# A macaron block of two feed-forward layers and a scan: the opening in another order

## The reference

```python
def ffn(x):                                   # weights w1, w2, h1, h2, w3 hold -1, 0 and 1
    h = silu(tlin(x, w1, s1)) * tlin(x, w2, s2)          # 128 -> 512
    h = gelu(tlin(h, h1, sh1), approximate=False)        # 512 -> 512
    h = gelu(tlin(h, h2, sh2), approximate=False)        # 512 -> 512
    return tlin(h, w3, s3)                               # 512 -> 128
x = x + 0.5 * ffn(layernorm(x))
x = x + attn(layernorm(x))                    # h_t = tanh(B x_t + A h_(t-1)), then C and W_out
x = x + 0.5 * ffn(layernorm(x))
```

## Time and profile before

| | |
|---|---|
| median of 3 runs | 384.37 us (384.05 to 384.40) |
| the profiled execution | 384.28 us, its span 382.4 us |
| granted clock of TensorE | 0.999 over the span |
| PE busy | 375.9 us, 98% of the span |
| DVE, ACT, POOL busy | 279.6, 267.7, 163.7 us |
| moved by DMA | 14.02 MB over the span |

### The profile page before, as it was taken

One profiled execution on the slowest core, in us unless ns is written; L12 is line 12 of the kernel. 1 busy time (PEld: TensorE's weight loads), 2 busy tenths in 40 slices (PEclk: granted clock), 3 DMA queues, 4 the chain that ended last, 5 costly groups with the idle time before them and its releaser, 6 DMA issues.

```text
span 382.4 us, 6587 instructions
## 1 busy us (share of the span) xinstructions
PE 375.9 (98%) x1793; PEld 299.9 (78%) x1793; DVE 279.6 (73%) x724; ACT 267.7 (70%) x625; POOL 163.7 (43%) x156
## 2 busy tenths in 40 slices
PE   7999999999999999999999999999999999999995
PEld 6877777778788787878778788888888788887774
DVE  5978989797777777576868866777767677686713
ACT  3899495768758688576685767858576775757654
POOL 3645362645526355242551633535334352533421
PEclk9999999999999999999999999999999999999999
DMA  7920000000000000000001001010100101000001
GB/s 228 433 112 1 27 2 27 2 2 28 2 28 0 2 27 0 28 2 28 27 2 56 2 18 39 0 55 2 46 9 0 55 0 55 0 29 27 2 28 33
DMA packets 6366, 14.02 MB, mean 37 GB/s; under 512 B 1088, under 2 KB 2112, under 8 KB 6080
## 3 DMA queue, kind: packets, MB, share of 16 engines
q1 hardware_dynamic: 5328, 13.37, 9.2%
q10 hardware_dynamic: 1008, 0.29, 0.3%
HBM read 7.37 MB, written 2.10 MB: 25 GB/s over the span
## 4 chain that ended last, share of the span: by engine, by line
PE 85%; issue 7%; POOL 3%; ACT 3%; DVE 2%; POOLq 0%; DVEq 0%
PE F L274 66%; PE FR L274 7%; PE FR L302 2%; PE SC L491 2%; POOL y_lo L1489 1%; PE SC L422 1%; POOL y_lo L1495 1%; PE F L519 1%; PE FR L292 1%; ACT y_hi L1216 1%; PE SC L274 1%; ACT y L1213 1%; PE MI L302 1%; PE F L521 1%; PE MI L282 1%
## 5 line engine op out<-in xcount | busy, mean ns | idle before, releaser
L274 PE MATMUL F<-y_hi,w_hi 128*128 128x512 f32 (+1 forms) x484 | 196.7, 407 | 0.3 <-DVE y_lo L1045 0.2
L274 PE MATMUL F<-y_lo,w_hi 128*128 128x512 f32 (+1 forms) x484 | 188.5, 390 | 0.0
L274 PEld LDWEIGHTS F<-y_hi,w_hi 128*128 128x128 f32 x484 | 91.0, 188 | 20.6 <-issue 2.2
L1213 ACT ACTIVATE y<-F,sc 128x512 f32<-128x512 f32 x111 | 76.1, 685 | 41.4 <-PE F L274 40.3
L274 PEld LDWEIGHTS F<-y_lo,w_hi 128*128 128x128 f32 x484 | 91.2, 188 | 15.9
L837 DVE TENSOR_TENSOR y_lo<-y,y_hi 128x512 fp32r<-128x512 f32 x79 | 64.9, 821 | 39.1 <-ACT y_hi L1216 39.1
L1489 POOL TENSOR_TENSOR y_lo<-y,y_hi 128x512 fp32r<-128x512 f32 x48 | 66.7, 1396 | 59.3 <-DVE y_hi L824 48.6
L1495 POOL TENSOR_TENSOR y_lo<-y,y_hi 128x512 fp32r<-128x512 f32 x48 | 62.5, 1308 | 34.8 <-ACT y_hi L1216 34.5
L1216 ACT ACTIVATE y_hi<-F,sc 128x512 fp32r<-128x512 f32 x111 | 76.0, 684 | 0.0
L1232 ACT ACTIVATE h<-SC 128x32 fp32r<-128x32 f32 x96 | 18.7, 195 | 47.9 <-PE SC L437 46.9
L274 PE MATMUL F<-xn_hi,w_hi 128*128 128x512 f32 x118 | 49.5, 420 | 0.1
(11 more groups left out here) (170 smaller groups left out, 438.4 us busy)
## 6 DMA issues: line engine op xcount, KB each, us to landing
x_all<-in_xT SPq DMA_DIRECT2D x1, 2048.0 KB, 15.6
x_all<-x1c SPq DMA_DIRECT2D x8, 256.0 KB, 2.3
x_all<-lnin SPq DMA_DIRECT2D x8, 256.0 KB, 2.2
out<-outb SPq DMA_DIRECT2D x7, 256.0 KB, 2.0
x_all<-in_xtok SPq DMA_DIRECT2D x1, 1536.0 KB, 11.4
w_raw<-in_h1T SPq DMA_DIRECT2D x2, 512.0 KB, 6.9
w_raw<-in_h2T SPq DMA_DIRECT2D x2, 512.0 KB, 8.2
x_all<-in_xtok SPq DMA_DIRECT2D x2, 128.0 KB, 2.6
```

The costliest lines, as they stand in the source:

```text
L274: mm = nc.tensor.matmul(out, wtile(w, layer, k, m), y, start=first and i == 0, stop=last and i == len(pairs) - 1)
L1213: nc.scalar.activation(y23[:, m, :], bankt[:, :], ACT.Gelu, scale=s)
```

## The change

Six things change, all of them in the opening.

- The number of zero matmuls, WARM, goes from 19 to 15.
- w1 and w2 are laid out by output tile, tile m of w1 beside tile m of w2, in one array w12T. Its first piece is now 256 columns (m = 0), its second the other 768. `wtile` finds the tiles there.
- The second half of chunk 0 is loaded by ACT's queue, ahead of ACT's small loads. Three small loads that the scan needs (`a_raw`, `b_rep`, `mask`) go from ACT's queue to the end of SP's.
- On DVE, `count(0)` goes from ahead of chunk 0's normalisation to behind it, and `count(1)` from ahead of `xn_lo` to behind chunk 1's statistics.
- On ACT, only piece 0 is cast ahead of `xn_hi`; piece 1 is cast behind it in two parts; the cast of h1's first half goes behind the first tanh, that of h1's second half behind chunk 1's normalisation.
- On POOL, `w_lo` of layer 1 is made in three parts (256, 256 and 512 columns) as the casts arrive, where it was two parts of 512.

```diff
-WARM = 19
+WARM = 15
...
-        PIECES = [(0, HID), (HID, HID)] + [(WOFF[2] + i * HALF, HALF) for i in range(4)] + [(WOFF[4], KT * P)]
+        PIECES = [(0, 2 * P), (2 * P, 2 * HID - 2 * P)] + [(WOFF[2] + i * HALF, HALF) for i in range(4)] + [(WOFF[4], KT * P)]
...
         def wtile(w, layer, k, m):
 
+            if layer < 2:
+                off = (2 * m + layer) * P
+                return w[:, off:off + P]
...
-                pe.wait_ge(w_hi_ready, 2)
+                pe.wait_ge(w_hi_ready, 1)
                 pe.wait_ge(xn_hi_r, 1)
...
             first_layer1()
+            pe.wait_ge(w_lo1_ready, 2)
             layer1(0, 1, True)
-            pe.wait_ge(w_lo1_ready, 2)
+            pe.wait_ge(w_lo1_ready, 3)
             layer1(0, 2, True)
...
             first_layer2(1)
+            pe.wait_ge(w_hi_ready, 5)
             first_layer2(2, range(KT - 1))
...
-            count(0)
             dve.wait_ge(rstd["f"], 1)
...
-            count(1)
+            count(0)
             dve.wait_ge(xn_hi_r, 1)
...
             first_stats(1)
             mean_negated(1)
+            count(1)
             count(2)
...
+            act.dma_start(xt_all[:, N // 2:N], xtok[:, N // 2:N]).then_inc(ld_x0[1], 16)
             act.dma_start(ident[:, :], ident_d).then_inc(ld_id, 16)
...
-            act.dma_start(a_raw[:, :], Ablk).then_inc(ld_scan, 16)
-            act.dma_start(b_rep[:, :], Brep).then_inc(ld_scan, 16)
-            act.dma_start(mask[:, :], mask_d).then_inc(ld_scan, 16)
...
             hi_part(0)
-            hi_part(1)
             act.wait_ge(feat_first, 1)
...
-            hi_part(2)
+            hi_part(1, slice(0, 2 * P))
+            hi_part(1, slice(2 * P, None))
...
             layer1(0, 0)
-            hi_part(3)
+            hi_part(2)
             layer1(0, 1)
...
             normalise(1, beside_normalisation)
+            hi_part(3)
             layer1(0, 3)
...
-            for half in range(2):
...
-                pool.tensor_tensor(part[0], part[1], part[2].bitcast(F32), ALU.subtract).then_inc(w_lo1_ready, 1)
+            for i, (lo, hi) in enumerate(((0, 2 * P), (2 * P, 4 * P), (4 * P, 2 * HID))):
+                pool.wait_ge(w_hi_ready, i + 1)
+                pool.tensor_tensor(w_lo[:, lo:hi], w_raw[:, lo:hi], w_hi[:, lo:hi].bitcast(F32),
+                                   ALU.subtract).then_inc(w_lo1_ready, 1)
...
-            for i in range(2):
-                sp.dma_start(xt_all[:, i * N // 2:(i + 1) * N // 2], xtok[:, i * N // 2:(i + 1) * N // 2]).then_inc(ld_x0[i], 16)
-            for i, (w, lo, hi) in enumerate(((w1T, 0, HID), (w2T, 0, HID), (h1T, 0, HALF), (h1T, HALF, 2 * HALF),
-                                             (h2T, 0, HALF), (h2T, HALF, 2 * HALF), (w3T, 0, KT * P))):
+            sp.dma_start(xt_all[:, 0:N // 2], xtok[:, 0:N // 2]).then_inc(ld_x0[0], 16)
+            for i, (w, lo) in enumerate(((w12T, 0), (w12T, 2 * P), (h1T, 0), (h1T, HALF), (h2T, 0), (h2T, HALF), (w3T, 0))):
...
             sp.dma_start(x_all[:, :], xT).then_inc(ld_xall, 16)
+            sp.dma_start(a_raw[:, :], Ablk).then_inc(ld_scan, 16)
+            sp.dma_start(b_rep[:, :], Brep).then_inc(ld_scan, 16)
+            sp.dma_start(mask[:, :], mask_d).then_inc(ld_scan, 16)
```

More of the change, by code:

```diff
@@ L56, in wait, with build @@
     engine.wait_ge(sem, value)
-def build(nc, xT, xtok, w1T, w2T, h1T, h2T, w3T, scales, Ablk, Brep, CTrep, WoutT, ident_d, mask_d, outT):
+def build(nc, xT, xtok, w12T, h1T, h2T, w3T, scales, Ablk, Brep, CTrep, WoutT, ident_d, mask_d, outT):
     with ExitStack() as ctx:
@@ L549, in first_turn @@
                 layer1(1, 1, gen)
-                pe.wait_ge(w_hi_ready, len(PIECES) - 1)
+                pe.wait_ge(w_hi_ready, len(PIECES))
                 pe.wait_ge(w3_hi_ready, 1)
@@ L1378, in count, with hi_part @@
                                      accum_out=ne_cnt[:, i:i + 1]).then_inc(ne_act, 1)
-            def hi_part(i):
-                off, width = PIECES[i]
+            def hi_part(i, cut=slice(None)):
                 act.wait_ge(ld_w[i], 16)
+                lo, hi, _ = cut.indices(PIECES[i][1])
+                off, width = PIECES[i][0] + lo, hi - lo
                 nc.scalar.copy(w_hi[:, off:off + width], w_raw[:, off:off + width]).then_inc(w_hi_ready, 1)
+            act.dma_start(xt_all[:, N // 2:N], xtok[:, N // 2:N]).then_inc(ld_x0[1], 16)
             act.dma_start(ident[:, :], ident_d).then_inc(ld_id, 16)
@@ L1537, in _ @@
             pool.wait_ge(normed["f"], 1)
-            pool.wait_ge(ld_w[0], 16)
-            pool.wait_ge(ld_w[1], 16)
-            pool.wait_ge(w_hi_ready, 2)
-            for half in range(2):
-                part = [w[:, 0:WOFF[2]].rearrange("p (l n) -> p l n", l=2)[:, :, half * HID // 2:(half + 1) * HID // 2]
-                        for w in (w_lo, w_raw, w_hi)]
-                pool.tensor_tensor(part[0], part[1], part[2].bitcast(F32), ALU.subtract).then_inc(w_lo1_ready, 1)
+            for i, (lo, hi) in enumerate(((0, 2 * P), (2 * P, 4 * P), (4 * P, 2 * HID))):
+                pool.wait_ge(w_hi_ready, i + 1)
+                pool.tensor_tensor(w_lo[:, lo:hi], w_raw[:, lo:hi], w_hi[:, lo:hi].bitcast(F32),
+                                   ALU.subtract).then_inc(w_lo1_ready, 1)
             inverse_std("f", 1, mv_f, ve_f, rs_f)
@@ L1550, in _ @@
             with pool.If(is_general != 0):
-                pool.wait_ge(w_hi_ready, len(PIECES) - 1)
+                pool.wait_ge(w_hi_ready, len(PIECES))
                 pool.wait_ge(w3_hi_ready, 1)
@@ L1598, in _ @@
                 off, width = PIECES[i]
-                sp.dma_start(w_raw[:, off:off + width], w[:, lo:hi]).then_inc(ld_w[i], 16)
+                sp.dma_start(w_raw[:, off:off + width], w[:, lo:lo + width]).then_inc(ld_w[i], 16)
             sp.dma_start(xt_all[:, 2 * N:], xtok[:, 2 * N:]).then_inc(ld_x, 16)
             sp.dma_start(x_all[:, :], xT).then_inc(ld_xall, 16)
+            sp.dma_start(a_raw[:, :], Ablk).then_inc(ld_scan, 16)
+            sp.dma_start(b_rep[:, :], Brep).then_inc(ld_scan, 16)
+            sp.dma_start(mask[:, :], mask_d).then_inc(ld_scan, 16)
             def save_x1(k):
@@ L1662 @@
         "xtok": np.ascontiguousarray(x.reshape(CHUNKS, QT, P, P).transpose(2, 0, 1, 3)).reshape(P, -1),
-        "w1T": tiles(v["ffn_w1_w"]), "w2T": tiles(v["ffn_w2_w"]), "h1T": tiles(v["ffn_h1_w"]),
+        "w12T": np.ascontiguousarray(np.stack([tiles(v[n]).reshape(P, KT, P) for n in ("ffn_w1_w", "ffn_w2_w")],
+                                              axis=2)).reshape(P, -1),
+        "h1T": tiles(v["ffn_h1_w"]),
         "h2T": tiles(v["ffn_h2_w"]), "w3T": tiles(v["ffn_w3_w"]),
```

## The result

The changed kernel takes 385.74 us (385.24 to 386.68, 15 runs), the kernel before 384.37 (383.46 to 385.17, 15 runs): the ratio is 1.0041, 95% interval 1.0030 to 1.0051. It is slower by 1.4 us; the forecast was 384.5 and its range ended at 385.1. The profiled execution took 385.53 us with a span of 383.2.

The account below looks back on a forecast made before the run. PE, busy 98% of the span, is gated at L742 by `ne_sum`, which DVE's and ACT's queues set. 0.07 (Step 2) + 0.14 (Step 3) = 0.2 us later, so 384.5 us forecast, range 383.9 to 385.1.

Parts of the forecast that it names:

- Step 1: Start of layer 1: earlier normalisation and fewer zeros end `xn_hi` at 8.36, 0.8 us sooner, bounds 0.4 to 0.9.
- The zeros' term: PE's opening: four fast zero matmuls fewer free PE 0.92 us sooner, at 7.17; 0.85 of it taken.
- The input's landing: Chunk 0's first half, both halves issued at once: lands 0.05 us later, bounds no change to 0.45.
- Step 2: DVE's queue up to the first gate: `count(1)` adds 0.87 us, so the gate comes at 12.45, 0.07 later.
- Step 3: ACT's queue from first `y_hi` to last count: cast adds 0.94 us, 0.80 absorbed, leaving 0.14 (0.04 to 0.24).
- Step 4: PE: waits about 0.7 us within layer 2 for the third `y`, and another 0.4 at L742 for `ne_sum`.
- The gain coming through: Rival, 5%: the 0.8 us of the earlier layer 1 start reaches the end, giving 383.5.
- The clock's rival: TensorE's pace falls at PE's wait for `xn_hi` after fewer zeros: 1.3 us later, 385.6; chance 5%.
- late input: First half lands as late as the second, 0.45 us on Step 1: 384.9 to 385.0; some 15%, within the range.

Follow-up runs that it names:

- scales_behind: The changed kernel with the three small DVE instructions on the scales put behind chunk 0's normalisation and `count(0)`, no transfer moved; 385.18 us, 1.0019 to the kernel before.
- before_scales_late: The kernel before with the load of the scales issued behind ct and wout on ACT's queue, fourth instead of second; 385.47 us, ratio 1.0040.
- one_queue: The changed kernel with the second half of chunk 0 back on SP's queue, behind the first; 384.78 us, 1.0008 to the kernel before.
- casts_back: scales_behind with the casts of h1's two halves back in their earlier places; ran once, only its trace used: ACT 8.20 us against 8.28.
- before_15_zeros: The kernel before with 15 multiplications of zeros instead of 19, nothing else; 383.89 us, ratio 0.9992.
- scales_first: The changed kernel with the load of the scales issued first on ACT's queue, ahead of chunk 0's second half; 385.69 us, 1.0033 to the kernel before.

## Why the prediction was wrong

**Step 1 failed.** The prediction had the normalisation start at 6.25 "with the count behind it", and `xn_hi` end at 8.36. It names `rs_f` and `count(0)` as what DVE waits for, and overlooks what stands between the statistics and the normalisation in the same queue: `s1h`, s3h and s12h, which wait for the scales. Before, that wait was over at 4.0 and invisible. The change moves the scales behind 128 KB on ACT's queue, and the prediction, though it followed the input's half and the three scan loads, never asked what was queued behind the half. Of the 0.92 by which the normalisation came later than forecast (7.17), `rs_f` explains 0.23 (6.44 instead of 6.21) and the wait on the scales the other 0.69. `xn_hi` ended at 9.07: 0.71 late. scales_behind and before_scales_late show the wait from both sides, and one_queue shows that the second queue makes it.

**The zeros' term was mis-sized too, hidden behind that.** Step 1 had the four zeros that go as fast ones, so that PE would be free at 7.17. In the changed kernel's trace the last of the 15 starts at about 7.23, so PE is free at about 7.46, which the late normalisation hides; in one_queue PE is free only at 7.81, and there it counts. So this term was 0.3 to 0.6 short in these two traces. That the zeros last longer in one execution than in another isn't in the prediction.

**The input's landing was mis-sized.** 0.05 was taken, with 0.45 as bound; the statistics started 0.31 later (3.70), and in the other kernels with the half first on ACT's queue from 3.87 to 3.98, against 3.15 to 3.56 in the kernels with both halves on SP's queue. The rule of the Trainium skill that was weighed there (DMA: Bandwidth & Descriptors, "Issuing engines are not separate DMA queues": transfers of several issuing engines share the 16 engines, so a second queue only saves issue time) was the better guide: the second half landed at 3.84, no sooner than before, and the first at 3.65. The same page of the Trainium skill ("Queues, rings and completion order") says that an engine works a ring off in order and takes turns between queues. The scales agree: 2.4 us to landing in first place on ACT's queue, 2.5 to 3.0 in second place behind `ident`, 4.6 to 5.2 in third behind the half and `ident`.

**Step 2 was right in its main term** (0.87; measured 0.86) and 0.22 short: `nmean` took until the count's start 0.29 instead of 0.07, beside POOL's last part of `w_lo`.

**Step 3 was right**: 0.14 predicted, 8.29 - 8.26 = 0.03 measured here, 0.08 between scales_behind and casts_back. One reading ahead of it was a tie: the `y_hi` at 13.88 was said to wait for the first `y` (13.84), but the tanh ahead of it on ACT ended only then too (13.25 + 0.69 = 13.94, with the overlap of 0.1). In the changed kernel it waits for `y` alone, 1.05 us.

**Step 4 was right in kind.** PE waits in layer 2 for the third `y`, and at the gate. The gate decides: `ne_sum` came 1.02 later instead of 0.2, which is 0.71 + 0.22 - 0.11 more, and past the branch all is 0.99 later. By the last layer it is 1.1; the last save gives 0.25 back (its issue on SP takes 1.30 us instead of 1.55), so the span is 0.8 longer.

**The time outside the span was put at nothing, without a reason.** The prediction let the whole time move with the gate. The profiled executions differ by 1.25 and the medians by 1.37, and 0.4 of that lies outside the span. In the medians of all runs it is 1.9 us for the kernel before, before_15_zeros and before_scales_late, 2.3 to 2.4 for the changed kernel and those made from it with the half on ACT's queue, and 2.1 to 2.2 with the half back on SP's. So it differs from kernel to kernel, and some 0.2 of the 0.4 goes with the second queue; the cause is open.

**The rivals.** The gain coming through did not happen, since no gain was made. In before_15_zeros, where no count had been put in its way, an earlier start did reach `ne_sum`. The clock's rival gave 385.6, and that this is close to the time measured is luck, for its reason isn't there: behind PE's wait matmuls start 0.23 apart (9.53, 9.76), and before_15_zeros loses nothing. That a load on DVE's path is late was weighed only as a late input, never for the scales.

With the half back on SP's queue the time is 384.78, within the forecast's range. That the edits to the order make and spend about the same fits this: what they leave can't be told from nothing (0.9996 to 1.0021). It is not shown step by step, since in that run's one trace the zeros held `xn_hi` to 8.87 and `ne_sum` to 23.06. The second queue makes most of the loss: 0.96 of the 1.37, 0.8 of it in the span.

## What to carry to other kernels

When a transfer is put ahead on a queue, list what is queued behind it, and for each of these the first instruction that waits for it and all that stands behind that instruction on its engine: in before_scales_late a 9 KB load cost 1.1 us. A wait that the trace of before doesn't show, since it was over in time, is not a wait that is gone; give each its slack. And an earlier start is worth only what the next gate's own queues leave of it: here a count of 0.87 on DVE would have taken all of the 0.8 forecast. And a trace covers only the span: hold the time outside it against that of before, too.

## What the runs showed of the hardware that was not expected

- The same 15 multiplications of zeros took 5.09 to 6.50 us in the profiles of kernels that begin alike. They start some 0.43 us apart at first, the level of 1.2 GHz, and 0.23 apart later, that of 2.4 GHz; how many are slow differs from execution to execution, and the zeros' end, at times the transposes, with it. The profile's granted clock reads 1.00 from 2 to 8 us of the changed kernel all the same.
- Two TENSOR_SCALARs of DVE on 4 columns took longer beside POOL's subtraction, and ended when it ended: `s1h` 0.58 us in scales_behind, until 8.70, with POOL's first part of `w_lo` until 8.67, and 0.17 in the changed kernel, where POOL was idle; `nmean` 0.37 in the changed kernel, until 11.47, with POOL's last part until 11.45, and 0.17 before. DVE's BATCH_NORM_AGGREGATE beside that same last part kept its 0.18.
- With a 9 KB load ahead of a 128 KB one on ACT's queue (scales_first), the latter landed about 1 us later (4.8 instead of 3.84), though its issue moved by only 0.45; the 128 KB on SP's queue landed 0.7 sooner (2.95 instead of 3.65).
